# Moving one half of every second block of score maxima behind the value products on TensorE, in an attention and expert kernel

## The reference

```python
x = conv_attention(x)                      # 1x1 projections, softmax over 1024 x 1024 scores, + x
t = tokens(x)
t = t + attention(layer_norm(t))           # group norm, qkv, 8 heads of 32 channels, projection
t = t + experts(layer_norm(t))             # 8 experts, one a token, gelu between two layers
```

```python
scores = einsum('bnhd,bmhd->bhnm', q, k) / sqrt(32)     # 1024 x 1024 a head
attn   = softmax(scores, axis=-1)
vals   = einsum('bhnm,bmhd->bnhd', attn, v)
```

## Time and profile before

| what | value |
|---|---|
| median of 3 runs | 1209.71 us |
| range of the runs | 1205.38 to 1212.19 us |
| profiled execution, its time | 1209.87 us |
| profiled execution, its span | 1208.0 us |
| mean granted TensorE clock over the span | 0.951 |
| busy TensorE matmuls, share of the span | 1109.3 us, 92% |
| busy VectorE, share of the span | 709.2 us, 59% |
| busy GpSimd, share of the span | 674.5 us, 56% |
| busy ScalarE, share of the span | 469.8 us, 39% |

### The profile page before, as it was taken

The page is one execution under the profiler, slowest core; times in us unless marked ns, Lnnn a source line. Parts: engine busy times, 40 slices in busy tenths (PEclk is TensorE's granted clock), DMA queues, the critical chain, the costliest instruction groups (busy, mean ns, idle before and its releaser), DMA issues. The chain is left out here.

```text
span 1208.0 us, 24384 instructions
## 1 busy us (share of the span) xinstructions
PE 1109.3 (92%) x7846; PEld 822.0 (68%) x7847; DVE 709.2 (59%) x1523; ACT 469.8 (39%) x556; POOL 674.5 (56%) x686
## 2 busy tenths in 40 slices
PE   6899999898669999999999999998966999999995
PEld 3577877677445555555555555556745999999995
DVE  3364747575647777777777777752561644444442
ACT  2303232311225555555555555564641222323221
POOL 0155353452227777777777777781064445555553
PEclk8899999899779999999999999999976999999998
DMA  7335665436161323232323232314598565666661
GB/s 215 96 116 173 211 211 188 184 124 229 62 217 33 99 65 96 64 97 64 99 62 98 64 98 63 97 53 133 197 322 219 170 216 196 220 210 214 216 204 58
DMA packets 69676, 173.66 MB, mean 144 GB/s; under 512 B 12768, under 2 KB 33184, under 8 KB 68992
## 3 DMA queue, kind: packets, MB, share of 16 engines
q1 hardware_dynamic: 55760, 130.73, 34.0%
q0 software_dynamic: 13296, 41.84, 10.3%
q10 hardware_dynamic: 576, 0.53, 0.3%
HBM read 117.16 MB, written 52.45 MB: 140 GB/s over the span
## 5 line engine op out<-in xcount | busy, mean ns | idle before, releaser
L225 DVE TENSOR_REDUCE s_nmax<-ps_v 128x1 f32<-128x512 f32 x484 | 311.5, 685 | 115.0 <-PE ps_v L219 105.3
L1083 POOL TENSOR_TENSOR h_added<-h_added,h_expd 128x1024 f32<-128x1024 f32 x124 | 295.5, 2383 | 38.1 <-ACT h_expd L1106 30.2
L1106 ACT ACTIVATE h_expd<-ps_v 128x1024 f32<-128x1024 f32 x128 | 131.0, 1024 | 157.0 <-PE ps_v L1132 152.3
L1975 PE MATMUL ps_h<-xs_c,lnt 128*128 128x128 f32 x1248 | 149.9, 280 | 4.4 <-DVE xs_c L1912 4.4
L1975 PEld LDWEIGHTS ps_h<-xs_c,lnt 128*128 128x128 f32 x1248 | 146.6, 196 | 5.3 <-issue 2.9
L1146 PE MATMUL h_ps_o<-h_expd,s_vh 128*32 128x256 f32 x2048 | 137.3, 386 | 0.0
L1106 ACT ACTIVATE h_expd<-h_ps_e 128x1024 f32<-128x1024 f32 x128 | 130.4, 1019 | 0.0
L648 PE MATMUL a_ps_v<-a_val,a_expd 128*128 128x257 f32 x512 | 119.7, 387 | 5.3 <-ACT a_expd L519 4.5
L2026 ACT ACTIVATE hid<-ps_h 128x1024 f32<-128x1024 f32 x39 | 39.9, 1024 | 195.4 <-DVE ps_h L1905 195.4
L1829 POOL TENSOR_TENSOR pause<-pause 128x1 f32<-128x1 f32 x156 | 49.6, 318 | 116.6 <-DVE ys L1930 89.2
L648 PEld LDWEIGHTS a_ps_v<-a_val,a_expd 128*128 128x128 f32 x512 | 97.8, 193 | 23.6 <-ACT a_expd L519 6.5
(11 more groups left out here) (256 smaller groups left out, 2024.9 us busy)
## 6 DMA issues: line engine op xcount, KB each, us to landing
lnt<-in_w SPq DMA_DIRECT2D x39, 1024.0 KB, 5.0
qk_scr<-a_head_hi SPq DMA_DIRECT2D x16, 512.0 KB, 3.9
qk_scr<-a_head_lo SPq DMA_DIRECT2D x16, 512.0 KB, 5.5
a_w_qk<-in_w POOLq DMA_DIRECT2D x24, 256.0 KB, 4.1
w_scr<-a_w_hi POOLq DMA_DIRECT2D x24, 256.0 KB, 2.4
w_scr<-a_w_qk POOLq DMA_DIRECT2D x24, 256.0 KB, 3.1
w_hi<-w_scr SPq DMA_DIRECT2D x8, 768.0 KB, 4.5
w_lo<-w_scr SPq DMA_DIRECT2D x8, 768.0 KB, 9.9
```

The costliest lines, as they stand in the source:

```text
L225: self.nc.vector.tensor_reduce(self.nmax[k][:, nb, half:half + 1], ps_m[:, half, :], AX.X, ALU.max, negate=True).then_inc(self.v_max, 1)
L1083: nc.gpsimd.tensor_tensor(total[:, :], (expd[:, 0, :] if m == 1 else total[:, :]), expd[:, m, :], ALU.add).then_inc(g_add, 1)
L1106: nc.scalar.activation(expd[:, m, :], flat(ps_e[m % 2]), ACT.Exp, scale=SCALE).then_inc(a_exp, 1)
L1975: last = nc.tensor.matmul(ps_h[k][:, c // 4, c % 4 * P:(c % 4 + 1) * P], w1_now[k][:, t, c * P:(c + 1) * P], xs_c[:, t, :], start=(t == 0) ...
```

## The change

`maxima` takes a list of halves, and the order on TensorE is changed for the second block of each pair (block 2c+1). Its half 0 stays ahead of the values. Its half 1 now stands behind them: in pair 0 behind the tail and ahead of `max_turn`, in pair 1 behind `all_sums`, in pairs 2 and 3 behind the values. There it is directly ahead of half 0 of the next pair's first block (or, in pair 0, of `max_turn`). The number of instructions, the order of the halves among themselves, the waits of each and the streams of the other engines are as before.

```diff
-    def maxima(self, pe, ps_m, g, s, nb, first=False):
+    def maxima(self, pe, ps_m, g, s, nb, first=False, halves=range(2)):
...
-        for half in range(2):
+        for half in halves:
...
-                    def step_maxima(i):
+                    def step_maxima(i, halves=range(2)):
...
-                            hd.maxima(pe, ps_m, NB * h + LEAD + i, (j + ahead) % SLOTS, (i + LEAD) % NB)
+                            hd.maxima(pe, ps_m, NB * h + LEAD + i, (j + ahead) % SLOTS, (i + LEAD) % NB, halves=halves)
...
                         step_maxima(2 * c)
                         step_scores(2 * c)
                         step_scores(2 * c + 1)
-                        step_maxima(2 * c + 1)
+                        step_maxima(2 * c + 1, (0,))
                         if c == 2 and not first:
                             outputs(t, j - 1)
                         if c == 0:
                             if not first:
                                 tail(j - 1)
+                            step_maxima(1, (1,))
+                            if not first:
 
                                 pe.wait_ge(v_norm, h)
                             if left >= 1:
...
                             if c == 1 and not first:
                                 all_sums(t, j - 1)
+                            step_maxima(2 * c + 1, (1,))
```

## The result

The changed kernel takes 1307.76 us (median of 4 runs, 1303.65 to 1309.83) against 1209.98 us for the kernel before (4 runs, one more than its table has). The ratio is 1.081, 95% interval 1.077 to 1.085: slower by 98 us, where 92 were forecast.

A forecast was written before the change was run, and what follows sets the result against it. TensorE alone was taken to set the pace in the heads. Terms of +0.57, +0.57, +0.03, +2.14 and -0.24 gave +3.07 us a round, 92 us in 30 rounds: 1302 us, range 1278 to 1322.

The forecast's parts named there:

- The hole: TensorE's idle time between the halves of a pair's second block; closing it would win 0.24 us a pair.
- O0 to values: From half 0 of a pair's second block to its values; put at 0.33 us, bounds 0.23 and 0.43.
- Pair 1: From the first block's half 0 to the second's half 1: 3.49 us against 3.73 before, -0.24.
- E1 behind O1: First block's half 1 waits until the preceding second block's half 1 is reduced: 1.28 us from start to start.
- E1 to the first score: From half 1 of a pair's first block to its first score; put at 0.34 us, bounds 0.23 and 0.43.
- Pair 1 to 2: From one second block's half 1 to the next pair's: 3.88 us against 3.31 before, +0.57.
- `max_turn` without the tail as cover: In pair 0, `max_turn` waits for the reduction and `least`: 1.58 us behind the second block's half 1.
- `norm`: In pair 3, on VectorE between two reductions, it would delay half 0 of the second block: +0.03 us.
- E0 behind `max_turn`: Half 0 of pair 1's first block was to start 0.03 us behind `max_turn`.
- The 130 waits: Weight loader's waits for reductions before the change, 53.4 us, taken as the gap between the second block's halves.
- The clock: TensorE's clock in the heads was expected to hold at 0.99, with some 82% busy.
- the rival that had 5%: Clock falls in the heads: if a tenth of the rounds fell, 36 us more, 1338 us and above; 5%.

The follow-up runs named there:

- x4: Changed kernel with half 1 of the first block moved behind the four scores in pairs 0, 2 and 3; 1272.49 us.
- x5: Changed kernel with each maxima reduction reading 256 of its 512 columns; 1259.25 us.
- x1: Kernel before, with the second block's half 1 moved behind the tail in pair 0 alone; 1239.59 us against 1209.52.
- x9: Changed kernel with `norm` behind block 6 instead of block 5; 1303.88 us.
- x6: Kernel before, in its old order, with each maxima reduction reading 256 of its 512 columns; 1174.23 us, ratio 0.972.
- x7: Kernel before, with pair 2's four output transposes between the halves of its second block; 1202.05 us, ratio 0.9955.
- x8: Kernel before, with two transposes between the second block's halves in each of pairs 2 and 3, `norm` behind block 7; 1196.23 us, ratio 0.9908.
- x10: Changed kernel with half 1 of the first block behind the scores in pairs 0, 2 and 3, and `norm` behind block 6; 1255.69 us.
- a1: Changed kernel run once more, unaltered, for its clock; 1306.78 us.

## Why the prediction was right

**The hole and its price.** O0 to values had no row before and was put at 0.33 us between two bounds; it is 0.33 us (662.59 to 662.92). Pair 1, where `row_lo` holds the values, was put at 3.49 us from E0 to O1 and is 3.49 (666.56 to 670.05).

**E1 behind O1.** 1.28 us forecast from three rows of the old order, 1.28 to 1.29 measured. x4 shows the cause by moving E1, x5 by shortening what it waits for. E1 to the first score is 0.34 us as put (653.01 to 653.35). Pair 1 to 2 is 4.31 us (651.73 to 656.04), which is 3.74 before (616.62 to 620.36 in the earlier trace rows) and the forecast +0.57.

**`max_turn` without the tail as cover.** 1.58 us forecast; 1.49 (646.65 to 648.14, from O1 to `max_turn`) and 1.58 us (664.78 to 666.36) measured. By x1 this part of the change, with the hole of pair 0 won, is 30 us of the 98.

**Two small terms were too small.** The round is 18.22 us here instead of 18.06. `norm` was put at +0.03 us; pair 2 to 3 takes 3.99 us (656.04 to 660.03) instead of the 3.91 that 3.31 + 0.57 + 0.03 give. O0 comes 2.56 us behind O1 there (656.04 to 658.60), as in pair 0 (660.03 to 662.59), but its weights are loaded only then, because the loader stands until E0's reduction ends:

```profile
658.60 0.19 PEld L219 LDWEIGHTS ps_v<-s_stk2m,s_stk2n 96*128 96x128 f32 x1 [0.29 <-DVE s_nmax L225]
```

The values came 0.43 us behind it instead of 0.33; x9 moves `norm` and gets the 0.33 back. And E0 behind `max_turn` was put at 0.03 us as in the earlier trace rows; it is 0.09 (648.14 to 648.23) and 0.20 (666.36 to 666.56). What E0 waits for there is not settled: the trace names nothing. The 0.16 us a round are 5 us in 30 rounds, most of what lies between 92 and 98.

**A reading that was off.** The 130 waits of the list before are five a round, and only four of them are the holes. The fifth is the weight loader's idle time ahead of E0 of a round, while TensorE still runs the values; in x6, where the holes are closed, 26 waits with 10.7 us are left. The sum did not rest on that list.

**The clock** held in the changed kernel, in three profiles, with TensorE busy for 85% of the heads where 82% were forecast. The rule of the Trainium skill that was weighed ("TensorE: Matmul & The Clock Gate", section "A second HAM failure mode: psum-queue depth-cycling") is not borne out by these three. Two of the experiments show such a swing of the clock, in three and in two rounds, as the last section tells.

## What to carry to other kernels

With one buffer for each half, moving a producer later moves it nearer to its buffer's next user. Before such a move, add up the chain from producer to consumer to next producer, and count what is left on the engine between the two; here 0.57 us were left of a chain of 1.28. An instruction that stands behind long work may be covering a chain for the instruction after it, as the tail did for `max_turn`, and such cover shows in no list of waits. A small hole is better filled with work that needs neither buffer, as the transposes in x7 and x8, than by moving one of the two that need it.

## What was not expected of the hardware

The clock fell in single stretches of the heads in x9 (three times) and x10 (twice), and in none of the three profiles of the changed kernel, whose waits are nearly the same. One of them in x9, by the windows around it (the clock is the third number from the end), and by the values of pair 1 in it and one round later:

```profile
524.00:528.00 4.00, 3.33 (x38) 1.62 (x36) 1.92 (x3) 1.94 (x2) 1.46 (x1) 1.00 0.00 0
...
530.40:533.80 3.40, 3.25 (x26) 1.41 (x26) 0.84 (x3) 1.82 (x3) 2.53 (x2) 0.53 0.12 41
```

TensorE's rows:

```profile
530.66 1.94 PE L1146 MATMUL h_ps_o<-h_expd,s_vh 128*32 128x256 f32 x16 [0.15 <-DVE s_mrow_lo L252]
...
550.31 1.07 PE L1146 MATMUL h_ps_o<-h_expd,s_vh 128*32 128x256 f32 x16 [0.18 <-DVE s_mrow_lo L252]
```

The values take 1.94 us instead of 1.07 at the lower of the two levels, 1.2 GHz, and the round 19.65 us (530.66 to 550.31) instead of 18.1. The wait of `max_turn` and that of these values lie just ahead of it, but the same wait in the other rounds left the clock alone. So the rival that had 5% is not far off: in orders with these waits the clock can fall, at 1.5 us a time, for a part of a round, rather than as a steady loss. Both orders in which it fell have `norm` behind block 6, and no trace with `norm` behind block 5 shows a fall between its first round and the end of the heads, the changed kernel's three included. By the expectation of a1 that speaks for `norm`'s new place, but with one trace of each of the two orders it is not shown. What decides it in one round and not in the next stays open.
